# Group 7 joins the groups that get x2 by a product of the scaled diagonal, and each such product becomes four of 128 columns

## What is computed

```python
x = x + L0_ffn(L0_cond(x, cond))   # mixing weights by a small MLP, then a quantised gated FFN with low-rank parts
x = x + L1_ffn(L1_cond(x, cond))   # a grouped convolution of 9 taps along the 512, then an fp8 linear layer
```

```python
x_scale = 448 / max(abs(z));  w_scale = 448 / max(abs(weight))
out = fp8(z * x_scale) @ fp8(weight * w_scale)
return x2 + out / (x_scale * w_scale)
```

## Time and profile before

| what | value |
|---|---|
| median of 3 runs | 373.33 us (373.03 to 373.79) |
| the profiled execution: its own time | 373.0 us |
| the profiled execution: its span, first to last instruction | 371.2 us |
| TensorE busy (PE) | 361.3 us, 97% of the span |
| VectorE busy (DVE) | 243.1 us, 65% |
| ScalarE busy (ACT) | 190.3 us, 51% |
| mean granted TensorE clock | 0.999 of full speed |
| last stage, from the first diagonal product to the last product | about 342.9 to 366.1 us of the span |

### The profile page before, as it was taken

How to read it: one execution, slowest core, us unless ns; L and a number is a source line. 1 busy time by engine, 2 the same in 40 slices (tenths; PEclk the granted TensorE clock), 3 DMA queues, 4 the chain that set the end, 5 groups by cost and what they waited for, 6 DMA issues and landing times.

```text
span 371.2 us, 5798 instructions
## 1 busy us (share of the span) xinstructions
PE 361.3 (97%) x2209; PEld 301.0 (81%) x2210; DVE 243.1 (65%) x409; ACT 190.3 (51%) x345; POOL 78.7 (21%) x68
## 2 busy tenths in 40 slices
PE   7999999999999999999999999999999999998994
PEld 3777887999888879998888789988888899997331
DVE  4949989436576664265766642737888822688995
ACT  5667797202656653035555641345667510066972
POOL 4000000021222332111422241113233221142040
PEclk9999999999999999999999999999999999999999
DMA  7997693495220000222200002326000299968288
GB/s 230 344 270 245 192 299 119 152 302 87 42 44 0 0 2 1 44 42 42 44 1 2 0 0 33 52 44 155 0 3 1 65 276 279 195 153 195 85 188 267
DMA packets 82476, 41.72 MB, mean 112 GB/s; under 512 B 52417, under 2 KB 72785, under 8 KB 82321
## 3 DMA queue, kind: packets, MB, share of 16 engines
q1 hardware_dynamic: 69072, 37.70, 37.4%
q10 hardware_dynamic: 12624, 1.82, 3.1%
q0 software_dynamic: 752, 1.84, 2.8%
HBM read 26.55 MB, written 14.80 MB: 111 GB/s over the span
## 4 chain that ended last, share of the span: by engine, by line
PE 93%; DVE 4%; ACT 1%; issue 1%; DVEq 0%
PE ps L675 44%; PE ps L660 25%; PE ps L690 6%; PE ps L608 4%; PE ps L710 3%; PE ps L870 3%; PE ps L666 2%; PE ps L712 2%; PE ps L850 1%; PE ps L623 1%; PE ps L568 1%; DVE v_plus L1506 1%; DVE q_fp L1525 1%; DVE amax L1383 0%; DVE v_plus L1513 0%
## 5 line engine op out<-in xcount | busy, mean ns | idle before, releaser
L660 PE MATMUL ps<-down_w,h_hi 128*128 128x288 f32 (+1 forms) x352 | 76.2, 297 | 0.0
L660 PE MATMUL ps<-down_w,h_lo 128*128 128x288 f32 (+1 forms) x352 | 74.7, 293 | 0.0
L675 PE MATMUL ps<-x_hi,gate_w 128*128 128x512 f32 (+1 forms) x176 | 69.9, 397 | 0.0
L675 PE MATMUL ps<-x_lo,gate_w 128*128 128x512 f32 (+1 forms) x176 | 69.6, 396 | 0.0
L675 PE MATMUL ps<-x_hi,up_w 128*128 128x512 f32 (+1 forms) x176 | 69.6, 396 | 0.0
L675 PE MATMUL ps<-x_lo,up_w 128*128 128x512 f32 (+1 forms) x176 | 69.3, 394 | 0.0
L1146 POOL TENSOR_TENSOR h_lo<-a_buf,h_hi 128x512 fp32r<-128x512 f32 (+1 forms) x33 | 42.7, 1295 | 90.0 <-ACT h_hi L984 90.0
L660 PEld LDWEIGHTS ps<-down_w,h_hi 128*128 128x128 f32 (+1 forms) x352 | 57.2, 189 | 1.1
L660 PEld LDWEIGHTS ps<-down_w,h_lo 128*128 128x128 f32 (+1 forms) x352 | 56.1, 188 | 0.0
L1435 DVE TENSOR_TENSOR a_buf<-a_buf,b_buf 128x512 f32<-128x512 f32 (+1 forms) x44 | 49.0, 1113 | 9.2 <-ACT a_buf L1050 8.1
L1157 POOL TENSOR_TENSOR x_nat<-y_buf,x_nat 128x512 f32<-128x512 f32 x15 | 20.8, 1385 | 117.0 <-DVE y_buf L1314 117.0
(11 more groups left out here) (196 smaller groups left out, 486.5 us busy)
## 6 DMA issues: line engine op xcount, KB each, us to landing
x_nat<-in_x SPq DMA_DIRECT2D x4, 1024.0 KB, 6.9
out<-x_nat SPq DMA_DIRECT2D x15, 256.0 KB, 4.5
turned<-x_nat SPq DMA_DIRECT2D x12, 256.0 KB, 3.3
x_nat<-in_down_q SPq DMA_DIRECT2D x11, 256.0 KB, 4.0
x_nat<-in_gate_q SPq DMA_DIRECT2D x10, 256.0 KB, 6.4
x_nat<-in_up_q SPq DMA_DIRECT2D x10, 256.0 KB, 6.6
edges<-zeros SPq DMA_DIRECT2D x4, 512.0 KB, 9.3
xt_own<-turned SPq DMA_DIRECT2D x6, 256.0 KB, 3.4
```

Source lines behind the costliest of these rows:

```text
L660: last = mm(ps[:, 4 + 2 * (j % 2) + m, 0:HALF + R], part[0:k, ic, j * P:(j + 1) * P], down_w[0:k, ic, m, :], start=first, stop=end)
L675: last = mm(ps[0:k, bank(ic, 2 * m), :], w[:, H * ic + c * k:H * ic + (c + 1) * k], part[:, c, :], start=c == 0 and part is x1_hi, stop=c ...
```

## The change

`FUSED` and `BEHIND_STEP` get group 7: its x2 now comes by a diagonal product behind step 2, so by `moved_by_act` ScalarE evicts it (line 1124) and VectorE no longer does (line 1536). And `add_input` makes four products over 128 columns each in place of one over 512, all with the same diagonal as weights and into quarters of the same bank; the first of them alone carries the start flag, and the last gives the semaphore. This holds for all groups in `FUSED`, eight now. HC is 4 and P is 128.

```diff
-FUSED = (4, 5, 6, 8, 9, 12, 13)
+FUSED = (4, 5, 6, 7, 8, 9, 12, 13)
 LEAD = (4,)
-BEHIND_STEP = {0: (5,), 1: (6,), 3: (8,), 4: (9,), 5: (12,), 6: (13,)}
+BEHIND_STEP = {0: (5,), 1: (6,), 2: (7,), 3: (8,), 4: (9,), 5: (12,), 6: (13,)}
...
                 if g >= 8:
                     wait_evicted(pe, g - 8)
-                mm(ps[:, g % 8, :], diag[:], x_nat[:, g, :], start=True, stop=False).then_inc(add_mm, 1)
+                for c in range(HC):
+                    at = slice(c * P, (c + 1) * P)
+                    last = mm(ps[:, g % 8, at], diag[:], x_nat[:, g, at], start=c == 0, stop=False)
+                last.then_inc(add_mm, 1)
```

## The result

The changed kernel takes 374.65 us in the median of 6 runs (374.05 to 374.83), the kernel before 373.33. The ratio is 1.0032, 95% interval [1.0022, 1.0042]: slower by 1.2 us, between 0.8 and 1.6. Forecast were 374.2 and "slower". The profiled execution took 374.83, with a span of 372.9; it is the slowest of the six, while the profiled one of the kernel before, 373.0, is among the fastest of its kind.

The account below looks back on a forecast made before the run. The last stage was taken as bound by VectorE until 350.78, then by TensorE alone; 0.62 for group 7 plus 0.25 for the pieces gave 373.33 + 0.87 = 374.2 us, range 373.0 to 374.9.

Parts of the forecast that it names:

- Group 7's product: TensorE behind step 2: a whole product of 1.06 us starts at 350.34 and delays step 3, +0.62 us.
- the hole ahead of step 3: TensorE idle between step 2's end at 350.34 and step 3's start at 350.78, 0.44 us.
- The pieces: Four pieces of 128 columns on TensorE: +0.036 us for each product, seven of which count, +0.25 us together.
- The decomposition: TensorE's product as one unhidden load of 0.105 us plus streaming passes: old 2 x 0.429, new 8 x 0.1117.
- Rival A: Seven products on TensorE's path: first load and gap behind hidden in part or whole, not slower, 373.6 to 373.0; chance 0.22.
- Rival B: TensorE's products: no load hides under a pass, +0.77 us each, +6.0 in all, 379.3 us; chance 0.04.
- Rival C: ScalarE's longer queue makes VectorE late for step 8 or the last evictions late, 0.61 on top, 374.8 us; chance 0.06.
- the evictions and writes behind it move along: Behind TensorE's last product: everything shifts with its 0.87 us delay, with nothing added.
- TensorE's part: Delay of TensorE's last product in the last stage: 0.62 + 0.25 = 0.87 us.

Follow-up runs that it names:

- the two leads: Kernel before with group 7 by a whole product, groups 4 and 5 ahead of step 0, 6 and 7 behind steps 0 and 1; 373.13 us, ratio 1.0000.
- group 8's adding DMA: Kernel before with group 7 by a whole product behind step 2 and group 8 written early and added to by DMA; 374.15 us, ratio 1.0018.
- kernel before with the fetches moved: Kernel before with the 17 clock-keeping products at the start cut into four of 128 columns; 374.95 us, ratio 1.0055.

## Why the prediction was right, and where it was short

- **Group 7's product: right.** Forecast +0.62 for what sticks out of the hole ahead of step 3; alone it gave a stage of +0.62. That it is the hole that decides, and not the product, the two leads show: the same eight products, placed into the two holes, cost nothing.
- **The pieces: right.** Forecast +0.036 for each product, measured 1.09 for 1.05 to 1.06, and in the stage 24.04 - 23.81 = 0.23 for the seven that count, 0.03 each. The decomposition held: one unhidden load (377 - 275 = 102 ns) for each product, and 275 ns passes behind it.
- **Rival A** (the edges of a product vanish) is refuted by the 377 ns of the first pass and by the 1.09. **Rival B** (no load hides) is refuted by the 64 loads under passes of 275 ns, eight of which take 1.09. The Trainium skill's sentence ("TensorE: Matmul & The Clock Gate", section "The mechanism"), that a load overlaps running products only where the row groups differ, doesn't hold for these full-height passes. The same section also has loads pulled ahead that go to a background weight buffer, which the prediction left out; no trace here names the buffer of a load. **Rival C** (ScalarE's longer queue) didn't happen: its scaling was done at 360.56, before VectorE came for it, and the end didn't grow when group 7 moved alone.
- **What it missed: "the evictions and writes behind it move along".** That step of the sum took the end for a constant. Without a fetch of instructions among the last writes it was one, 5.1 to 5.2 us, in all runs but that with group 8's adding DMA (5.6). The four pieces brought a hundred more instructions, and with them a fetch of TensorE's program into the last writes, which stretched the end from 5.1 to 5.9 us in the profiled execution. The forecast's 0.87 was the whole of TensorE's part (0.85). The measured 1.2 is this and some 0.35 behind TensorE, which the interval of the ratio lets be anything from nothing to 0.7. That the fetch makes the end longer is shown in the profiled executions; that the 0.35 is all its work is argued. So the direction was forecast by the right mechanism. But TensorE's part alone is only 0.1 above the 0.75 us that can be told from no change, and that the change came out clear of it is in part the luck of the fetch. The Trainium skill ("Runtime: NRT & Kernel Launch", section "Instruction fetch mechanics") says that instructions are fetched in blocks of 16 KiB and that crossing a boundary is mostly hidden. The size agrees with the trace (0.28 MB in 17 packets). The hiding isn't complete here: TensorE's chain has no wait for the block, but the writes end later.

What stays open is the fetch's price to better than a few tenths, why a pass of 128 columns costs more beyond its columns than one of 256, what made the other executions with group 8's adding DMA slower than the profiled one, and what cost the two kernels with cut products at the start their microseconds ahead of the last stage.

## What to carry to other kernels

Cutting an fp32 product into pieces that share their weights saved nothing here: every piece loaded them again, under the passes, and eight passes of 128 columns took 0.03 us longer than two of 512. Work added to an engine is priced by the hole it falls into, so find the holes and move the work there, before asking whether the work could be cheaper. And if a kernel ends in writes that keep all DMA engines busy, count the instructions too: here some 30 to 100 more put one more fetch into the last writes.

## What was not expected of the hardware

A fetch of 16 KB of TensorE's instructions is a single packet, among the data on the same 16 DMA engines. In the last writes one engine then finished alone, at 25 to 41 GB/s against some 390 of all, for 0.5 to 1.25 us after the others. Whether that costs time depends, as far as three executions show it, on the gap in the traffic that follows. With the pieces alone the packet took 1.0 us, the gap was long enough, and the end stayed at 5.2. In the changed kernel it took 1.9 us and the late engine filled the whole gap (end 5.9). In the kernel before with the fetches moved it took 1.0 us, but there was hardly a gap (end 6.0). And taking 0.50 us off the binding engine gained nothing where the writes that follow had no gap left.
